# The clip of the exponentials of slots 3 to 15 is done by GpSimd instead of VectorE

## The reference, cut to what matters

```python
proj = jnp.einsum('bhtd,rhdm->rbhtm', zn, omega)
poly = proj ** 2 * inv_sqrt_m
exp_arg = jnp.clip(proj * sqrt_2s - s, -20.0, 20.0)
prf = jnp.exp(exp_arg) * inv_sqrt_m
fused = poly * prf * sqw
```

## Time and profile before

| what | value |
|---|---|
| median of three runs | 1404.43 us (1402.59 to 1406.11) |
| span of the profiled execution | 1402.6 us |
| PE busy | 1130.2 us (81%) |
| DVE busy | 1066.6 us (76%) |
| ACT busy | 907.3 us (65%) |
| POOL busy | 411.7 us (29%) |
| mean granted TensorE clock | 0.911 |
| DVE clip, L1103 | 57.8 us in 128 instructions |

### The profile page before, as it was taken

How to read it: one execution, slowest core, us unless ns; L and a number is a source line. 1 busy time by engine, 2 the same in 40 slices (tenths; PEclk the granted TensorE clock), 3 DMA queues, 4 the chain that set the end, 5 groups by cost and what they waited for, 6 DMA issues and landing times. The chain is left out here.

```text
span 1402.6 us, 17119 instructions
## 1 busy us (share of the span) xinstructions
PE 1130.2 (81%) x5421; PEld 623.9 (44%) x5421; DVE 1066.6 (76%) x1672; ACT 907.3 (65%) x1781; POOL 411.7 (29%) x349
## 2 busy tenths in 40 slices
PE   3875988898878987798888988798888987775865
PEld 1433444444544454444544455444544454433533
DVE  1755568877997799887997789877897788855654
ACT  3542679567785769566785769567785768447631
POOL 3010006520354006520354006520354005422641
PEclk8986899899999999999999999999999999886895
DMA  2000001100020102101120002100010002101100
GB/s 72 1 8 0 19 13 61 38 1 32 31 67 9 32 1 68 38 1 32 31 61 16 31 1 68 38 0 32 31 53 16 32 1 60 38 6 41 60 23 8
DMA packets 31401, 41.11 MB, mean 29 GB/s; under 512 B 4617, under 2 KB 14674, under 8 KB 31314
## 3 DMA queue, kind: packets, MB, share of 16 engines
q1 hardware_dynamic: 31314, 40.02, 9.2%
HBM read 37.65 MB, written 2.36 MB: 29 GB/s over the span
## 5 line engine op out<-in xcount | busy, mean ns | idle before, releaser
L611 POOL TENSOR_TENSOR read<-state,c_row 128x1024 f32<-128x1024 f32 x128 | 300.1, 2356 | 303.9 <-DVE state L1120 108.7
L1120 DVE TENSOR_TENSOR_SCAN state<-decay,bank 128x512 f32<-128x512 f32 x256 | 296.1, 1203 | 61.5 <-PE bank L1438 52.3
L1454 PE MATMUL bank<-read,ident 128*128 128x512 f32 x512 | 262.9, 643 | 1.1 <-POOL read L611 1.1
L1438 PE MATMUL bank<-ident,drive_by_token 128*128 128x128 f32 x1024 | 166.2, 299 | 111.3 <-DVE state L1120 96.3
L705 ACT ACTIVATE drive_by_token<-dtu_t,b_t 128x256 f32<-128x256 f32 x512 | 217.0, 497 | 7.2 <-PE bank L1438 7.1
L693 ACT ACTIVATE decay<-dt,neg_a 128x510 f32<-128x510 f32 x256 | 169.5, 712 | 65.8 <-DVE state L1120 65.7
L1438 PEld LDWEIGHTS bank<-ident,drive_by_token 128*128 128x128 f32 x1024 | 122.6, 151 | 177.3 <-issue 114.8
L1379 PE MATMUL bank<-znt,omega 128*128 128x512 f32 x256 | 144.8, 649 | 18.3 <-ACT sqf L684 18.3
L1130 DVE TENSOR_TENSOR s_sb<-bank,causal 128x512 f32<-128x512 f32 x128 | 87.9, 687 | 76.6 <-PE bank L1392 76.5
L681 ACT ACTIVATE expf<-bank,minus_s,root2s 128x512 f32<-128x512 f32 x128 | 99.5, 777 | 64.6 <-PE bank L1379 63.6
L1454 PEld LDWEIGHTS bank<-read,ident 128*128 128x128 f32 x512 | 99.3, 211 | 87.2 <-issue 81.5
(11 more groups left out here) (237 smaller groups left out, 1723.4 us busy)
## 6 DMA issues: line engine op xcount, KB each, us to landing
c_row<-c_rows SPq DMA_DIRECT2D x128, 256.0 KB, 3.1
xa<-x_dram SPq DMA_DIRECT2D x8, 256.0 KB, 3.7
out_dram<-x SPq DMA_DIRECT2D x8, 256.0 KB, 2.3
omega<-omega_t_dram SPq DMA_DIRECT2D x1, 512.0 KB
c_rows<-xdbl SPq DMA_DIRECT2D x8, 32.0 KB, 1.6
wqkv<-w_qkv_t_dram SPq DMA_DIRECT2D x1, 192.0 KB
state<-w_down_dram SPq DMA_DIRECT2D x1, 176.0 KB, 2.3
state<-w_gate_dram SPq DMA_DIRECT2D x1, 128.0 KB, 2.1
```

The costliest lines, as they stand in the source:

```text
L611: pool.tensor_tensor(read[:, s % STATE_BUFFERS], state[:, s % STATE_BUFFERS], c_row[:, s % C_BUFFERS].unsqueeze(1).broadcast_to([P, DT, TO ...
L1120: dve.tensor_tensor_scan(state[:, s % STATE_BUFFERS, c], decay[:, s % 2, c].rearrange("p b t -> p (b t)"), bank[:, DRIVE_BANK + c], 0.0, A ...
L1438: last = pe.transpose(bank[:, DRIVE_BANK + c, t * P:(t + 1) * P], by_token[:, s % DRIVES, t, c * P:(c + 1) * P], ident[:])
L1454: last = pe.matmul(bank[:, 6 + k], ident[:], read[:, s % STATE_BUFFERS, k], start=(s == 0), stop=(s == STATES - 1))
```

## The change

In slots 3 to 15 the clip of `expf` is issued by POOL, in its turn after `deviation` of the mid group; slots 0 to 2 stay on DVE. The operation reads and writes the same tile with the same bounds. DVE now waits for the semaphore `clipped` of POOL where it waited for its own. On POOL `deviation` of the old group stands behind the clip of slot 5 and ahead of that of slot 6.

```diff
+CLIPS = 3
...
+            def clip(ga, s):
+
+                pool.wait_ge(exp_done.sem, exp_done.at(ga, s + 1))
+                pool.wait_ge(clipped.sem, clipped.at(ga, s))
+                pool.tensor_scalar(expf[:, s % 2], expf[:, s % 2], EXP_HIGH, EXP_LOW,
+                                   ALU.min, ALU.max).then_inc(clipped.sem, 1)
+
...
-                if turn.has_old:
-                    deviation(ffn_b.norm, turn.old)
+                for k in range(SLOTS):
+                    if turn.has_new and k >= CLIPS:
+                        clip(turn.new, k)
+                    if turn.has_old and k == 5:
+                        deviation(ffn_b.norm, turn.old)
...
-                dve.wait_ge(exp_done.sem, exp_done.at(ga, s + 1))
-                dve.tensor_scalar(expf[:, s % 2], expf[:, s % 2], EXP_LOW, EXP_HIGH,
-                                             ALU.max, ALU.min).then_inc(clipped.sem, 1)
+                if s < CLIPS:
+                    dve.wait_ge(exp_done.sem, exp_done.at(ga, s + 1))
+                    dve.tensor_scalar(expf[:, s % 2], expf[:, s % 2], EXP_LOW, EXP_HIGH,
+                                      ALU.max, ALU.min).then_inc(clipped.sem, 1)
                 dve.wait_ge(clipped.sem, clipped.at(ga, s + 1))
                 dve.wait_ge(sq_done.sem, sq_done.at(ga, s + 1))
```

## The result

The changed kernel takes 1386.9 us, the median of 4 runs (1385.46 to 1388.4), against 1405.27 for the kernel before on the same chip: a ratio of 0.986, with an interval of 0.984 to 0.989. That is 18.4 us faster; 10.2 us were forecast. The profiled execution took 1385.46 us and its span is 1383.9. A few executions in a slow state (such as one of 1604.6 us at a granted clock of 0.641, with slot 6 alone on POOL) are left out of all times and ratios here.

What follows compares the result with a forecast made beforehand. PE was taken as nearest to full, with DVE's time counting only where PE waits for it. 1.2 + 0.05 + 0.45 = 1.7 us per half, over six halves 10.2 us, gave 1394 us; range 1383 to 1406.

Steps and rivals of the forecast that it cites:

- the forecast's own band: Whole time between 1389 and 1400 us, with a chance of 0.52.
- POOL's clip: POOL's 128x512 one-input pass was taken to last 0.7 us, between 0.42 and 1.27.
- first rival: POOL's clip costs 1.27 us instead of 0.7; 6.6 us lost, 1411; chance 0.13.
- Place A: Second layer norm, up to PE's transposes: earlier statistics and an unhindered `deviation` gain 1.2 us net per half.
- slot 6's wait for its clip: Second layer norm: slot 6's multiplication waits for the clip behind `deviation`, so cannot hold its last step; 0.5 us.
- the gain of slot 7's clip: Inside the rounding, DVE loses this clip, 0.45 us; the way through mask, ACT and PE does not get it.
- meetings: POOL's clips and DVE passes hold each other up on SBUF, 0 or 0.15 to 0.65 us each.
- Place B: Hidden layer: the clips of slots 11 and 12 give 0.9 us, less meetings of 0.4 and 0.45, leaving 0.05.
- Place C: End of the half, leading into the next scan: slot 15's clip leaves DVE, 0.45 us per half.
- cover of slot 9: Shortest lead found: 1.15 us for POOL's pass of 0.7 and two semaphores, so DVE's multiplication would not wait.
- second rival: Every meeting on SBUF costs a whole clip; 4.2 us gained in all, 1400; chance 0.21 with its neighbours.
- third rival: Shorter PE waits keep the granted clock up behind Place A; 10 us more gained, 1384; chance 0.14.

Runs made afterwards that it cites:

- filler run: Six short matmuls that nobody reads added in PE's waits of Place A: to the kernel before, 1405.0 us; to the changed kernel, 1386.4 us.
- folded kernel: Changed kernel without clip instructions in slots 3 to 15: upper bound in DVE's multiplication, weight in ACT's square, lower bound left out; 1372.0 us, ratio 0.977.

## Why the prediction was right, and what was off

The range held, and the gain comes from the places that the prediction named; but nearly half of it was not forecast. Some 3 us of that are in the terms below. The other 5 have no cause shown here; without them the time would lie in the forecast's own band.

**POOL's clip.** Taken at 0.7 us from two shorter rows; it takes 0.61. The upper bound, 1.27, was far too high, and with it the first rival. Even a clip of twice the length broke about even.

**Place A.** Booked 1.5 us for the rounding; it came 1.48 earlier, though by the clip of slot 5 alone: the 0.5 put down to slot 6's wait for its clip was not needed. But only 1.2 net was booked ahead of PE, and 37.78 - 36.13 = 1.65 was measured. What was wrong in this term is the way that was taken to end last: I let mask, ACT and PE set the transposes, without the gain of slot 7's clip and with 0.3 for meetings. At the transposes both ways end together: before, PE waited 0.15 us for DVE, and after, its own work ends within 0.1 of the rounding's end. What decides is the way behind them. The filler run shows that transposes 0.67 later cost nothing, and that PE next waits for ACT, which had waited for the mask behind the rounding. So the end of the rounding sets the time, and it had the gain of slot 7's clip: from the first reduction to the transposes it takes 7.08 us, where it took 7.24 before and with slot 5 alone. That is 0.45 for the clip of slot 7, less 0.29 for the meeting of slot 8. The meeting of slot 7 cost nothing in this execution; in other halves with the same instructions it cost 0.46, as shown above. So the 0.3 booked for meetings was about right, on the other way.

**Place B.** Booked 0.9 less 0.4 and 0.45; the meetings cost 0.40 and 0.38, and from `b_ffn_xq` to `b_ffn_h` the half is 23.85 - 23.72 = 0.13 shorter, where 0.05 was booked. The prices were taken from near the middle of 0.15 to 0.65, for want of the time at which the passes arrive, so that they came out so near is in part luck. **Place C.** Booked 0.45; (83.25 - 61.63) - (80.95 - 59.85) = 0.52. **Elsewhere** nothing was booked, and the runs on slots 3, 4, 9 and 10 and on turns 0 and 1 gave nothing. Six of DVE's nine waits for POOL are those of slot 6, 0.53 us each. The cover of slot 9 held in four of the six halves only: in the two without a fall its multiplication waits 1.11 us for POOL. The 1.15 us of cover were read in a half with a fall. It costs nothing here, since the next mask on DVE waits for PE and comes as early as the rest.

**The second rival**, that each meeting costs a whole clip, had the mechanism right and the size wrong. In the three large meetings of the changed kernel (L1039, L1004 and the multiplication of slot 12), DVE's pass comes 0.24, 0.07 and 0.02 us after POOL's and ends as late as if it had started at 632.95, 652.83 and 656.54, that is, 0.15, 0.14 and 0.22 before POOL's recorded end. So it is held for nearly all that is left of POOL's pass, and then runs at its own speed: 0.29 to 0.40 lost in each. The Trainium skill, SBUF — State Buffer, section "Who interferes with whom", says that the order of issue decides who blocks, that a VectorE instruction with two SBUF inputs contends with GpSimd's reads, and that one with a single SBUF input outside the two-port modes does not. The trace agrees: DVE's mask, which reads PSUM and one tile of SBUF, came 0.02 us behind POOL's clip of slot 3 and kept its 0.69 us, where the multiplication of slot 12, with two inputs from SBUF and as far behind, took 1.13:

```profile
609.51 0.62 POOL L653 TENSOR_SCALAR expf<-expf 128x512 f32<-128x512 f32 x1 [7.07 <-ACT expf L692]
609.53 0.69 DVE L1142 TENSOR_TENSOR s_sb<-bank,causal 128x512 f32<-128x512 f32 x1 [1.62 <-PE bank L1404]
```

**The sum, and the third rival.** 1.7 us a half was forecast and 2.2 to 2.3 measured, 13.1 to 13.8 us in all: some 3 of the 8 us that were missing, 2.7 of them in the term of place A (1.65 for 1.2). The other 5 don't show in the marks of these halves, and slots 3, 4, 9 and 10 and turns 0 and 1 gave nothing. The measured time lies in the third rival's band, and the clock may have a part in them: the falls behind place A are gone in two of the six halves, and the full-clock time lost in the six attention halves of the profiled executions, the sum of (1 - granted clock) times length, fell from 23.9 to 13.7 us (14 falls and 8). But the filler runs show that this can't simply be added: falls taken away there, before or after the change, left the whole time where it was. Single executions with the same instructions differ by as much as the missing 5 us (1381.7 to 1388.7 from turn 2 on), and where the falls come is not explained by any run here. That part stays open.

## What to carry to other kernels

Moving work off a busy engine pays where another engine's chain of waits ends on it, and nowhere else: of 13 clips moved, one alone gave 1.45 of the 2.2 us, because it changed which of two engines came first, and four gave nothing. Price an engine that shares its memory with the old one by the meetings in the new order, read off the timeline one by one; and where two passes become ready at the same moment, book either outcome (0 or 0.46 us here). A way that ends last at one place is to be followed on to the next wait, before it is taken for the one that counts. Compare stretches at equal granted clock before believing that a few us of the whole time are a gain of the change.

## What was not expected of the hardware

The folded kernel without its last three clips did less work and took some 14 us more, with halves that are no longer, at a mean granted clock of 0.898 instead of 0.924 in the profiled executions: more than any single step of this change was worth. Matmuls added in PE's waits of the changed kernel removed every fall from the halves that held them, without shortening the kernel. And a step of 0.18 us on DVE took 0.64 in 3 of 6 halves of one execution and in none of another with the same instructions there, as POOL's pass started within 0.005 us of it.
